# Four-layer graph network: aggregation and GCN output placed right behind the third support matmul, value projection behind both, own buffers for the first support

## What is computed

```python
# block 0: mean aggregation
agg = adj @ x / max(sum(adj, -1), 1e-6)
x = layernorm(x + relu(concat([x, agg]) @ W.T))
# block 1: three GCN layers
h = relu(adj @ (x @ W1) + b1)
h = relu(adj @ (h @ W2) + b2)
x = layernorm(x + adj @ (h @ W3) + b3)
# block 2: attention, 8 heads of 64, mixed with adjacency and exp(-adj)
p = 0.33 * (softmax(q @ k.T / 8) + adj + exp(-adj))
x = layernorm(x + (p @ v) @ W_out + b_out)
# block 3: a gate by a softmax over the nodes
w = softmax(sum((q3 @ k3.T / 8) * adj, -1))
x = layernorm(x + w * v3)
```

## Time and profile before

| | |
|---|---|
| median of 3 runs | 1280.58 us (1278.61 to 1282.45) |
| the profiled execution's own time | 1280.6 us |
| its span in the profile | 1278.7 us |
| TensorE matmul busy (PE) | 1259.2 us, 98% |
| weight load busy (PEld) | 1156.0 us, 90% |
| VectorE busy (DVE) | 1155.8 us, 90% |
| ScalarE busy (ACT) | 958.4 us, 75% |
| GpSimd busy (POOL) | 177.2 us, 14% |
| mean granted TensorE clock | 0.998 |
| DMA | 49.06 MB, mean 38 GB/s |

### The profile page before, as it was taken

One profiled execution on the slowest core, in us unless ns is written; L12 is line 12 of the kernel. 1 busy time (PEld: TensorE's weight loads), 2 busy tenths in 40 slices (PEclk: granted clock), 3 DMA queues, 4 the chain that ended last, 5 costly groups with the idle time before them and its releaser, 6 DMA issues.

```text
span 1278.7 us, 30231 instructions
## 1 busy us (share of the span) xinstructions
PE 1259.2 (98%) x10732; PEld 1156.0 (90%) x10732; DVE 1155.8 (90%) x3671; ACT 958.4 (75%) x2534; POOL 177.2 (14%) x383
## 2 busy tenths in 40 slices
PE   8999999999999999999999999999999999999997
PEld 7888999999999999999999999999999999999886
DVE  6988999999999999999999999999999999998895
ACT  6677678778778787777787787787787787787773
POOL 0001111101111101111111111011111011111011
PEclk9999999999999999999999999999999999999999
DMA  6110111110111100111100111101111101110000
GB/s 230 35 35 2 35 43 44 44 31 14 44 43 44 43 27 19 43 44 43 44 12 34 43 44 44 43 2 43 44 43 44 43 2 44 43 44 10 10 9 25
DMA packets 42659, 49.06 MB, mean 38 GB/s; under 512 B 16272, under 2 KB 25232, under 8 KB 42512
## 3 DMA queue, kind: packets, MB, share of 16 engines
q1 hardware_dynamic: 42512, 47.14, 11.7%
HBM read 38.68 MB, written 8.39 MB: 37 GB/s over the span
## 4 chain that ended last, share of the span: by engine, by line
PE 94%; DVE 2%; ACT 2%; DMA 1%; issue 1%; POOL 0%; SPq 0%; POOLq 0%; DVEq 0%
PE psum L1551 63%; PE psum L1565 11%; PE psum L1803 9%; PE psum L1761 8%; PE psum L1854 1%; PE psum L1857 1%; ACT work L578 1%; DMA adjT_sb<-in_adjT 0%; DVE bn L929 0%; DMA v_sb<-in_w 0%; DVE x L963 0%; DVE x_pre L1021 0%; POOL rstd L382 0%; DVE x_pre L1187 0%; DVE work L1092 0%
## 5 line engine op out<-in xcount | busy, mean ns | idle before, releaser
L578 ACT ACTIVATE work<-work,shift 128x256 f32<-128x256 f32 x512 | 253.7, 500 | 4.9 <-DVE shift L1092 4.8
L1111 DVE SCALAR_TENSOR_TENSOR work<-work,rsum,extra 128x256 f32<-128x256 f32 x512 | 216.8, 475 | 1.0
L1092 DVE CUSTOM_DVE_ANT_0 work<-psum,minus_big 128x256 f32<-128x256 f32 x512 | 189.0, 417 | 3.0 <-PE psum L1761 2.8
L429 ACT ACTIVATE work<-psum 128x512 f32<-128x512 f32 x256 | 138.0, 598 | 71.6 <-PE psum L1565 71.5
L379 POOL TENSOR_TENSOR mv<-mv,eps 128x2 f32<-128x2 f32 x128 | 31.0, 242 | 1081.7 <-DVE mv L950 1081.7
L1551 PE MATMUL psum<-x2T_h,wqkv_h 128*128 128x256 f32 x512 | 145.6, 284 | 0.0
L429 ACT ACTIVATE sup_h<-psum 128x512 fp32r<-128x512 f32 x124 | 73.2, 590 | 95.2 <-PE psum L1551 95.1
L1551 PE MATMUL psum<-x2T_h,wqkv_l 128*128 128x256 f32 x512 | 143.0, 279 | 0.0
L1551 PE MATMUL psum<-x2T_l,wqkv_h 128*128 128x256 f32 x512 | 142.9, 279 | 0.0
L1565 PE MATMUL psum<-ident,work 128*128 128x128 f32 x1024 | 127.4, 273 | 0.0
L1803 PE MATMUL psum<-work,v_sb 128*64 128x256 f32 x1024 | 124.6, 385 | 0.0
(11 more groups left out here) (189 smaller groups left out, 3798.5 us busy)
## 6 DMA issues: line engine op xcount, KB each, us to landing
xT_sb<-in_xT SPq DMA_DIRECT2D x32, 256.0 KB, 2.6
adjT_sb<-in_adjT SPq DMA_DIRECT2D x32, 256.0 KB, 3.0
adj_sb<-in_adj SPq DMA_DIRECT2D x32, 256.0 KB, 4.0
x_sb<-in_x SPq DMA_DIRECT2D x32, 256.0 KB, 4.3
out<-y_sb SPq DMA_DIRECT2D x32, 256.0 KB, 3.5
work<-in_wqkv SPq DMA_DIRECT2D x1, 1536.0 KB, 9.6
mask_row<-in_nodemask SPq DMA_DIRECT2D x32, 32.0 KB, 4.2
w_raw<-in_w SPq DMA_DIRECT2D x3, 256.0 KB, 5.4
```

The costliest lines, as they stand in the source:

```text
L429: return nc.scalar.activation(dst, src, ACT.Copy, scale=scale)
L578: last = nc.scalar.activation(prob[:, p % 2, i, h], prob[:, p % 2, i, h], ACT.Exp, bias=shift[:, p % 2, h, i:i + 1], scale=-1.0, accum_out ...
L1092: last = V_.tensor_tensor_reduce(out=prob[:, p % 2, i, h], in0=bank(SCORES[p] + h)[:, i * N:(i + 1) * N], in1=minus_big[:, g % 2, i], scal ...
L1111: last = V_.scalar_tensor_tensor(out=prob[:, p % 2, i, h], in0=prob[:, p % 2, i, h], scalar=rsum[:, p % 2, h, i:i + 1], in1=extra[:, g % 2 ...
```

## The change

Four things change; matmuls, copies and subtractions stay the same in number and size.

1. TensorE's slot: `aggregate` HI and LO come first behind `support(2)`, then `gcn_out` HI and LO, then `values` HI and LO.
2. ACT's and DVE's slots are reordered to match; ACT's `first_graphs` has `sup0_hi(4)` earlier, DVE's `last_graphs` has `sup0_lo` and `sup_lo(2)` earlier.
3. From graph 3 on the first support has its own buffers `sup0`, and `sup0_hi` no longer waits for `gcn_out`.
4. To make room, the raw GCN weights (`w123_raw`) are loaded into parts of `work` and `x2_bout` that are unused at the start.

```diff
-        w123_raw = sb("w123_raw", [P, 3, FT, F])
+        sup0 = [sb(f"sup0_{s}", [P, NT, F], F32R) for s in "hl"]
...
+        w123_raw = [a.rearrange("p (k f) -> p k f", k=FT)
+                    for a in (work[:, 0, 3 * INNER:], work[:, 1, 3 * INNER:])] + [x2_bout[:, 1]]
...
+        def sup0_of(g):
+            return sup0 if g >= OWN_SUP0 else sup_of(g)
...
+        OWN_SUP0 = 3
...
             def sup0_hi(g):
                 if not live(g):
                     return
-                if g == 1:
-                    act.wait_ge(pe_sup0, once(g))
-                elif g == 2:
-                    act.wait_ge(pe_sup0, once(g))
-                else:
-                    reuse(act, pe_gcn, once(g - 1))
-                    act.wait_ge(pe_sup0, once(g))
-                copy(sup_of(g)[0][:, :, :], halves(bank(SUP0))).then_inc(act_sup0, 1)
+                act.wait_ge(pe_sup0, once(g))
+                copy(sup0_of(g)[0][:, :, :], halves(bank(SUP0))).then_inc(act_sup0, 1)
...
                 exps(s - 2, 1, 1)
+                adj_hi(s)
+                sup0_hi(s)
+                sup_hi(2, s - 1)
+                norm_apply(3, s - 5)
                 mask_bias(s - 1)
-                adj_hi(s)
-                norm_apply(3, s - 5)
-                sup_hi(2, s - 1)
-                sup0_hi(s)
+                self_copy(s)
                 values(s - 2)
-                self_copy(s)
...
                 recip_sums(s - 4, 1)
+                adj_lo(s - 2)
                 probs(s - 4, 1, 0)
+                sup0_lo(s - 2)
+                sup_lo(2, s - 3)
                 attention_out(s - 5)
-                adj_lo(s - 2)
-                sup_lo(2, s - 3)
                 norm_stats(2, s - 5)
-                probs(s - 4, 1, 1)
                 gcn_out(s - 3)
-                sup0_lo(s - 2)
-                norm_mean(2, s - 5)
                 norm_stats(1, s - 3)
                 norm_mean(1, s - 3)
                 aggregate(s - 2)
+                norm_mean(2, s - 5)
+                norm_apply(1, s - 3)
+                probs(s - 4, 1, 1)
                 relu_residual(s - 2)
-                norm_apply(1, s - 3)
...
                 support(2, s - 2, LO)
-                values(s - 3, HI)
+                aggregate(s - 1, HI)
+                aggregate(s - 1, LO)
                 gcn_out(s - 2, HI)
                 gcn_out(s - 2, LO)
+                values(s - 3, HI)
                 values(s - 3, LO)
-                aggregate(s - 1, HI)
-                aggregate(s - 1, LO)
```

More of the change, by code:

```diff
@@ L326, in load_w123 @@
             def load_w123(i):
-                sp.dma_start(w123_raw[:, i], w123_d[i]).then_inc(dma_w123[i], 16)
+                sp.dma_start(w123_raw[i], w123_d[i]).then_inc(dma_w123[i], 16)
             load_w0(0)
@@ L440, in w123_hi @@
                 act.wait_ge(dma_w123[i], 16)
-                weight_hi(w123[0][:, i], w123_raw[:, i])
+                weight_hi(w123[0][:, i], w123_raw[i])
             def wqkv_hi(k):
@@ L819, in first_graphs @@
                 adj_exp(4)
+                sup0_hi(4)
                 sup_hi(2, 3)
                 mask_bias(3)
-                sup0_hi(4)
                 values(2)
@@ L918, in w123_lo @@
             def w123_lo(i):
-                weight_lo(w123[1][:, i], w123_raw[:, i], w123[0][:, i], W1 + i)
+                weight_lo(w123[1][:, i], w123_raw[i], w123[0][:, i], W1 + i)
             def wout_lo():
@@ L1011, in sup0_lo @@
                 dve.wait_ge(act_sup0, once(g))
-                lo(sup_of(g)[1][:, :, :], halves(bank(SUP0)), sup_of(g)[0][:, :, :]).then_inc(dve_sup0, 1)
+                lo(sup0_of(g)[1][:, :, :], halves(bank(SUP0)), sup0_of(g)[0][:, :, :]).then_inc(dve_sup0, 1)
             def aggregate(g):
@@ L1379, in last_graphs @@
                 adj_lo(G - 1)
+                sup0_lo(G - 1)
+                sup_lo(2, G - 2)
                 attention_out(G - 4)
-                sup_lo(2, G - 2)
                 norm_stats(2, G - 4)
                 gcn_out(G - 2)
-                sup0_lo(G - 1)
                 norm_stats(1, G - 2)
@@ L1626, in aggregate @@
                     pe.wait_ge(dve_sup0, once(g))
-                last = nodes_product(bank(AGG), [a[:, g % ADJS] for a in adjT], sup_of(g), part, RIGHT_LATE)
+                last = nodes_product(bank(AGG), [a[:, g % ADJS] for a in adjT], sup0_of(g), part, RIGHT_LATE)
                 if part == LO:
```

## The result

The changed kernel takes 1288.95 us (median of 6 runs, 1287.45 to 1293.9) against 1279.58 us before (6 runs, 1278.61 to 1282.45): ratio 1.0071, 95% interval 1.006 to 1.0082. It is slower, by more than twice the 0.3% that counts as no change, and above the range forecast. Its profiled execution took 1289.04 us, with a span of 1287.1 us and a granted clock of 0.998, so both profiles ran at the upper clock level nearly throughout.

A forecast was written before the change was run, and what follows sets the result against it. TensorE, 98% busy, was taken as the bound, so only its losses between matmuls could be won. 1280.6 - 3.9 + 2.2 + 2.9 + 0.7 - 0.5 = 1282.0, with -0.2 for the pace 1281.8 us; range 1277.8 to 1286.2.

The forecast's parts named there:

- (a): Slots 6 to 31: waits at `x2_transpose` and `aggregate` go, -0.15 us per slot, -3.9 us in all (0 to -6.5).
- (d): End, once: `aggregate(31)` waits for `adj_lo(31)`, +0.7 us net; `gcn_out(31)` no longer waits for a support copy, -0.5 us.
- the pace: `gcn_out` and `aggregate` behind `support(2)` may keep its faster matmul spacing, up to -2.5 us; counted at -0.2 us.
- `aggregate`'s 0.03: Middle slots: `aggregate` HI no longer waits for the end of `gcn_out`, -0.03 us per slot.
- (b): Warm-up, once: `gcn_out(2, LO)` starts late because DVE does `sup0_lo(3)` ahead of `sup_lo(2, 2)`, +2.2 us (1.7 to 2.5).
- (c): Slot 5, once: DVE waits 2.4 us for GpSimd's two norms, and `aggregate(4)` for `adj_lo(4)`, +2.9 us (1.0 to 3.9).
- DVE setting the end of the slot: Rival, 16%: DVE reaches `scores(3)` 0.1 us or more later ahead of `tail_project`, 1284.6 to 1285.9 us.
- The port lock falling on DVE: Rival, 3%: GpSimd's shared port blocks DVE ahead of `x2`, 0.5 us in each middle slot, +13 us, 1295 us.

The follow-up runs named there:

- SP's edit: Changed kernel with SP issuing the small `gate_col` transfer ahead of the next graph's five loads instead of behind them: 1282.09 us, ratio 1.0014.
- the mended kernel: Changed kernel with `gate_col` ahead of loads, GpSimd's `norm_rstd` swapped, DVE's first slot as before, `adj_lo`/`sup0_lo` earlier in its second slot and at the end: 1275.58 us.

## Why the prediction was wrong, and where it was right

**(a), the middle slots: the step that failed is the moved `mask_bias`, costed at nothing.** The prediction followed DVE, TensorE and GpSimd, and put no price on the `mask_bias` that ACT does later; it appears only in (d), as something a copy no longer stands behind. It feeds SP's `load`, and `turn_gate_probs` is queued behind that load. The listing of ACT's order ahead of the prediction shows the row change places. What it delays is on none of the three engines that the prediction followed. Measured price: 9.3 us (the slots with and without SP's edit).

**The gain of (a) came out right, in part by luck.** With the new wait taken away the 26 slots give -4.02 us, where -3.9 and -0.2 for the pace had been forecast. Its largest part is what was said: the transposes take 0.11 us less in a slot. But `aggregate`'s 0.03 is not there in sum: the whole stretch from `aggregate` to `values` takes 5.61 us instead of 5.60. In its place 0.07 us a slot, 1.9 in all, came at `tail_project`, where the prediction expected nothing. In slot 10 its first two matmuls and the last row of `scores` ahead of them are, before and then with SP's edit:

```profile
337.14 0.09 DVE L1092 DVE_READ_ACCUMULATOR2_ANT shift<- 128x1 f32 x1
...
337.39 0.39 PE L1551 MATMUL psum<-w_h,x3T_h 128*128 128x384 f32 x1
337.62 0.34 PE L1551 MATMUL psum<-w_l,x3T_h 128*128 128x384 f32 x1
```

```profile
342.85 0.08 DVE L1092 DVE_READ_ACCUMULATOR2_ANT shift<- 128x1 f32 x1
...
343.23 0.34 PE L1551 MATMUL psum<-w_h,x3T_h 128*128 128x384 f32 x1
343.40 0.33 PE L1551 MATMUL psum<-w_l,x3T_h 128*128 128x384 f32 x1
```

DVE is done 0.30 us ahead instead of 0.16, and the two matmuls start 0.17 us apart instead of 0.23. The prediction had DVE just in time there, with a margin of 0 to 0.05 us; it is over 0.1. One reading was the wrong way round: `gcn_out` does not end 0.4 us later behind `support(2)`. By the prediction's own two durations, 1.83 leaving and 1.44 entering, it ends 0.4 us earlier, and the timelines show that (21.7 instead of 22.1 us into slot 10). DVE's `scores` row ends 0.23 us earlier in the slot.

**(b), warm-up: right in place, short in its consequence.** The start is 2.1 us late (2.2 forecast), and 0.3 us of it come back at `aggregate(3)`, as the prediction thought possible; from `hidden(0, 2)` at 68 us to slot 5 the changed kernel takes 42.84 us, the kernel before 41.02: +1.8. But the wait also hid 1.5 us of a second wait (`probs(1, 1, 1)`), and in four of five traces it brought 1.5 us of matmuls at the low clock level. The warm-up of the changed kernel's profile is longer by only 0.17 us because by 29 us it was 1.7 us ahead of the profile before. That lead is no gain of the change: in the profile before, TensorE's first matmuls start 0.21 us apart, the distance of the low level, from 7.3 to 11.1 us, and in the changed kernel's 0.12, which is 1.9 us. The start varies by itself: the kernel before and its four variants with the same warm-up lists have warm-ups of 106.74 to 109.84 us, and ACT's wait for the load of `wqkv` near 20 us, 0 to 3.1 us in them, is another part of that. The run with SP's edit had 2.8 us of this wait.

**(c), slot 5: right.** +2.8 for +2.9, with 2.49 us of DVE's idle time where 2.4 was forecast. GpSimd's order was undone alone; with `adj_lo(4)` moved up too, in the mended kernel, slot 5 is back at 38.88 us.

**(d), the end: right.** +0.77 and -0.62 for +0.7 and -0.5; the wait at `aggregate(31)` is 1.0 us, and 0.4 come back at `scores(29, ·)`, as forecast. With `adj_lo(31)` and `sup0_lo(31)` moved up, slot 32 falls to 38.61 us.

**The pace: the -0.2 us was not found, and what sets it is open.** `aggregate` and `gcn_out` kept the slower one (eight matmuls in 0.94 us) though they now follow `support(2)`. The mended kernel's middle slots are 1.1 us longer than those of the run with SP's edit alone, with no wait in the list that would explain it; why was not tried.

**The rivals.** The first, DVE setting the end of the slot, had the right place (`tail_project`) and the wrong cause: DVE was not late by its own work. What it rested on nearly held, that DVE has little to spare there: slot 10, with a wait of 1.76 us on DVE, is 1.7 us longer than the undisturbed slots. The port lock falling on DVE is not seen: DVE's norm rows are 0.73 us as before. GpSimd's rows show the longer durations still: its L395 takes 0.5 us on average, where the same row (L389) took 0.2 before.

**The sum.** Parts from the traces: -4.0 + 9.3 + 1.8 + 2.8 + 0.8 - 0.6 = +10.1 us. Less the lead of 1.7 us at the start this is the +8.4 of the two profiles; the medians say +9.4. The rest is within the spread of the warm-up. How often the low clock comes in the changed kernel's other runs is not known, since only one was profiled. The forecast's range was also added up wrongly at its low end: 1282.0 less 0.5 and 1.9 is 1279.6, not 1278. The result fell on the other side, above all of (a) eaten: the range allowed for a gain that fails, and not for a new wait.

## What to carry to other kernels

When an instruction moves, ask what its *completion* frees, not only who reads its result: here the last reader of a small buffer was what a load waited for, and behind the load, in one in-order queue, stood an unrelated transfer with a deadline. Put short transfers that someone waits for ahead of bulk loads whose own issue waits for something. And a wait can hide the next one: mend one at a time and read the trace again, as the 1.5 us behind the 2.0 us of idling in warm-up show. Last, a forecast that comes out right in sum can be made of parts that did not: compare it part by part.

## What was not expected of the hardware

- A transfer of 1 KB behind about 1 MB of loads in the same queue lands in 3.7 us (median), with none in front of it in 1.9 us.
- One DMA issue on SP took 1.18 us in slot 10, where its neighbours take 0.34 to 0.49.
- After dense work from 60 to 90 us (busy 9.9 to 10.0 us of every 10) TensorE idled for 2.0 us; in four of five traces the granted clock then fell (0.76, 0.50, 0.88 in three windows of 2 us with SP's edit alone), in the fifth it stayed at 1.00. It stayed there too behind the 1.5 us of idling at `probs(1, 1, 1)`.
- ACT waited 0 to 3.3 us for the load of `wqkv` near 20 us, from one trace to another, in kernels whose first loads are the same in size and order.
